# Non-local attention block: row products made over fewer steps, the next image's first products ended earlier, and left sums taken with transposes

## What is computed

```
x4  = groupnorm(x)                       # per image, 32 groups
g_x = g_w @ x4 + g_b                     # 128 x 4096
f   = x4.T @ x4                          # 4096 x 4096, symmetric
y   = softmax(f, axis=-1) @ g_x.T
wy  = W_w @ y.T + W_b                    # 256 x 4096
wy  = batchnorm(wy over all 4 images) * gamma + beta
out = x + wy + x4
```

## Time and profile before

| | before |
|---|---|
| median of 3 runs | 2225.02 us (2223.76 to 2226.59) |
| profiled execution's own time | 2227.25 us |
| its span, first to last instruction | 2225.5 us |
| mean granted TensorE clock | 0.982 of full speed |
| TensorE busy | 2082.0 us, 94% of the span |
| VectorE, ScalarE, GpSimd busy | 69%, 49%, 37% |

### The profile page before, as it was taken

One profiled execution on the slowest core, in us unless ns is written; L12 is line 12 of the kernel. 1 busy time (PEld: TensorE's weight loads), 2 busy tenths in 40 slices (PEclk: granted clock), 3 DMA queues, 4 the chain that ended last, 5 costly groups with the idle time before them and its releaser, 6 DMA issues.

```text
span 2225.5 us, 32504 instructions
## 1 busy us (share of the span) xinstructions
PE 2082.0 (94%) x9460; PEld 1487.4 (67%) x9460; DVE 1527.1 (69%) x3095; ACT 1096.3 (49%) x2234; POOL 813.5 (37%) x624
## 2 busy tenths in 40 slices
PE   5899999999999999999999999998999999999988
PEld 4687776755687777665668677675658777666433
DVE  5576666777766766686766666677776677667656
ACT  3344545556444444546544454555544444454645
POOL 3002223459502023447730222355950102345750
PEclk9999999999999999999999999999999999999989
DMA  3112233555512323464531223455541132336969
GB/s 137 76 76 87 99 114 128 166 152 166 185 45 90 112 74 109 142 199 133 174 106 78 86 100 114 128 175 155 172 167 62 72 119 90 119 119 222 333 234 359
DMA packets 108410, 304.53 MB, mean 137 GB/s; under 512 B 11584, under 2 KB 11968, under 8 KB 93888
## 3 DMA queue, kind: packets, MB, share of 16 engines
q1 hardware_dynamic: 108224, 302.30, 39.7%
HBM read 159.65 MB, written 142.61 MB: 136 GB/s over the span
## 4 chain that ended last, share of the span: by engine, by line
PE 67%; issue 11%; POOL 10%; DVE 4%; ACT 4%; DMA 3%; SPq 0%; DVEq 0%; POOLq 0%; ACTq 0%
PE bank L1199 11%; PE bank L1133 9%; PE bank L1135 9%; PE bank L1134 9%; PE bank L1175 8%; PE bank L1203 4%; PE bank L1205 4%; PE bank L1204 4%; POOL fy_d L694 4%; POOL fy_c L694 3%; PE bank L1349 3%; ACT ring L760 2%; PE bank L1270 2%; DMA fy_d<-spill 2%; POOL xl L667 2%
## 5 line engine op out<-in xcount | busy, mean ns | idle before, releaser
L786 ACT CAST phi<-bank 128x512 fp32r<-128x512 f32 x480 | 280.8, 587 | 779.0 <-PE bank L1175 778.4
L930 DVE TENSOR_SCALAR_CACHE_REDUCE ring<-bank 128x512 f32<-128x512 f32 x576 | 395.9, 687 | 245.2 <-PE bank L1135 200.4
L1133 PE MATMUL bank<-xh 128*128 128x512 f32 (+3 forms) x1152 | 521.2, 452 | 7.3 <-POOL xl L667 6.4
L1135 PE MATMUL bank<-xh,xl 128*128 128x512 f32 (+3 forms) x1152 | 439.1, 381 | 0.0
L965 DVE TENSOR_TENSOR plo<-bank,phi 128x512 fp32r<-128x512 f32 x480 | 325.7, 684 | 161.7 <-ACT phi L786 123.7
L1134 PE MATMUL bank<-xl,xh 128*128 128x512 f32 (+3 forms) x1152 | 436.4, 379 | 0.0
L1175 PEld LDWEIGHTS bank<-ident,ring 128*128 128x128 f32 x1920 | 233.6, 142 | 199.4 <-issue 130.0
L1175 PE MATMUL bank<-ident,ring 128*128 128x128 f32 x1920 | 295.5, 277 | 61.4 <-DVE plo L965 31.2
L760 ACT ACTIVATE ring<-ring,nmax 128x512 f32<-128x512 f32 x480 | 344.7, 720 | 0.0
L694 POOL TENSOR_TENSOR fy_c<-fy_c,maxrow 128x512 f32<-128x512 f32 x200 | 261.9, 1312 | 146.9 <-DMA fy_c<-spill 146.5
L694 POOL TENSOR_TENSOR fy_d<-fy_d,maxrow 128x512 f32<-128x512 f32 x188 | 243.0, 1295 | 190.4 <-DMA fy_d<-spill 190.3
(11 more groups left out here) (115 smaller groups left out, 2720.7 us busy)
## 6 DMA issues: line engine op xcount, KB each, us to landing
spill<-ring SPq DMA_DIRECT2D x112, 1024.0 KB, 4.4
fy_c<-spill SPq DMA_DIRECT2D x200, 256.0 KB, 4.6
fy_d<-spill SPq DMA_DIRECT2D x188, 256.0 KB, 4.2
ring<-x_dram SPq DMA_DIRECT2D x40, 512.0 KB, 4.6
lbuf<-spill SPq DMA_DIRECT2D x60, 256.0 KB, 3.8
yd<-yn SPq DMA_DIRECT2D x32, 256.0 KB, 3.4
fx_a<-x_dram SPq DMA_DIRECT2D x16, 512.0 KB, 8.6
out_dram<-fx_a SPq DMA_DIRECT2D x16, 512.0 KB, 5.4
```

What stands on the lines that cost most here:

```text
L786: nc.scalar.copy(phi[:, HI_BUF[n], :], whole(p)).then_inc(hi_made, 1)
L930: last = nc.vector.tensor_scalar(ring[:, SLOT[u], t, :], src, 1.0, None, ALU.mult, ALU.max, accum_out=rowm[:, t, c:c + 1])
L1133: nc.tensor.matmul(dst, xh[:, k, rows], xh[:, k, cols], start=(k == 0), stop=False)
L1135: last = nc.tensor.matmul(dst, xl[:, k, rows], xh[:, k, cols], start=False, stop=(k == K - 1))
```

## The change

Three things, and a part that follows from them:

- `plan_products` makes the products of block 2 in 19 steps in place of 25 (in block 1's steps), and those of blocks 3, 4 and 5 in 18. Blocks 1, 6 and 7 stay. As a result the last product of block 2 stands at step 1.21 (before 1.24), of block 3 at 2.17 (2.24), of block 4 at 3.21 (3.23), of block 5 at 4.17 (4.22); maxima are merged at 1.23, 2.19, 3.23, 4.19 (before 1.26, 2.26, 3.25, 4.24). Some steps hold two products: 1.03, 1.05, 1.14 to 1.18, 2.02, 2.08, 3.12, 3.13 (before: 1.14 to 1.16).
- `plan_exps` is not edited, but its bound moves: the four exponentials that stood together at 1.28 and 2.28 (three and one at 3.27 and 3.28) now stand one in each of the steps 25 to 28. The copy of the spread maxima (`take_maxrow`) moves from 1.29 to 1.26, from 2.29 to 2.27 and from 3.28 to 3.27.
- `NEXT_TO` is 239 in place of 245: the 32 products of the next image's row 0 stand at 181, 182, 184, ... 237, 239 (before 181, 183, 185, ... 242, 245), two of them moved from block 7 to block 6, and their maxima are merged at 7.16 (7.22). The sends to `spill` of their chunks move along; the one of chunk (0, 7) stands at 7.16 in place of 7.22.
- `sum_left` transposes the four 128 x 128 pieces of `lsb` against `ident` (128 columns each) in place of multiplying them by a 128 x 2 tensor of ones, and `invert` reduces the 128 x 512 result on VectorE into `lside` before it adds. The tensor `ones` and its memset go.

```diff
-        steps = range(PRODUCTS_FROM[j], PRODUCTS_FROM[j] + (25 if j < 6 else 2 * n))
+        steps = range(PRODUCTS_FROM[j], PRODUCTS_FROM[j] + {1: 25, 2: 19, 3: 18, 4: 18, 5: 18, 6: 2 * n, 7: 2 * n}[j])
...
-NEXT_AT, NEXT_TO = XN_STEP[0] + 5, TILES - 11
+NEXT_AT, NEXT_TO = XN_STEP[0] + 5, TILES - 17
...
-                    nc.vector.tensor_tensor(lsum[:, :], sps[:, 0:2 * T].rearrange("p (t o) -> p t o", o=2)[:, :, 0],
-                                            lsum[:, :], ALU.add).then_inc(summed, 1)
+                    nc.vector.tensor_reduce(lside[:, :], sps.rearrange("p (t m) -> p t m", t=T), AX.X, ALU.add
+                                            ).then_inc(side_summed, 1)
+                    dve.wait_ge(side_summed, b * (NB - 1) + j)
+                    nc.vector.tensor_tensor(lsum[:, :], lside[:, :], lsum[:, :], ALU.add).then_inc(summed, 1)
...
-                    last = nc.tensor.matmul(sps[:, 2 * t:2 * t + 2], lsb[:, t * P:(t + 1) * P], ones[:, :],
-                                            start=True, stop=True)
+                    last = nc.tensor.transpose(sps[:, t * P:(t + 1) * P], lsb[:, t * P:(t + 1) * P], ident[:, :])
```

More of the change, by code:

```diff
@@ L421, in nonlocal_block @@
         gavg = sb("gavg", [P, P])
-        ones = sb("ones", [P, 2])
         wgs = sb("wgs", [P, K, 2 * CI], F32R)
@@ L439, in nonlocal_block @@
         lsum = sb("lsum", [P, T])
+        lside = sb("lside", [P, T])
         linv = sb("linv", [P, T])
@@ L494, in nonlocal_block @@
         left_summed = sem("left_summed")
+        side_summed = sem("side_summed")
         summed = sem("summed")
@@ L698, in _ @@
             nc.gpsimd.memset(neghalf[:, :], -0.5)
-            nc.gpsimd.memset(ones[:, :], 1.0)
             nc.gpsimd.memset(ident[:, :], 0.0)
```

## The result

| | before | after |
|---|---|---|
| median beside each other | 2225.81 us (4 runs) | 2195.49 us (4 runs, 2194.60 to 2196.57) |
| ratio, 95% interval | | 0.9859 (0.9838 to 0.9880) |
| profiled execution's own time | 2227.25 us | 2195.28 us |
| its span | 2225.5 us | 2193.5 us |
| mean granted clock | 0.982 | 0.991 |

The change makes the kernel 1.4% faster, and the median is within 1 us of the predicted 2196.0. That it is so close is luck: the sum behind it was -29.2 us, the two profiled executions are 32.0 us apart and the two medians 30.3, and single terms of the sum were off by 3 to 5 us in opposite directions, as the point-by-point part shows. Each ratio is an estimate over the executions with its interval, and can differ from the quotient of the two medians by up to 0.001, or 2 us.

What follows compares the result with a forecast made beforehand. TensorE, 94% busy, was taken as the bound. Left sums with inverse -7.8, block ends -16.4, packed steps +2, clock -11, image ends +4 sum to -29.2: 2198.0 profiled, 2196 beside the median; forecast 2184 to 2207, wider range 2170 to 2216.

Steps and rivals of the forecast that it cites:

- What bounds the kernel: TensorE, 94% busy; time is won only where it does less, stands idle, or has a low clock.
- Ends of blocks: Steps 25 to 31 of blocks 1 to 3: holes fall from 7.6 to 3.5 us an image, -16.4 us.
- The rival that ScalarE bounds the longer ends: At block ends holes return in small pieces; only 8 us of holes and 4 of clock won, 2211; chance 0.14.
- Left sums: At 28 left sums, transposes take 0.45 us where ones and their matmul take 0.90: -12.6 us on TensorE.
- the rival by which transposes are no cheaper: Left sums: transposes pay by 128 columns, ones by 2; 12.6 us lost from the sum, 2208; chance 0.04.
- The inverse: VectorE's 0.75 us reduction delays it at step 5.01 of three images, +3.6, and in the last image's tails, +1.2.
- Packed steps: Products packed into earlier steps: VectorE at 79% holds, runs late only at 1.18 and 1.19; +2 us, 0 to +8.
- the slower rival: VectorE becomes the bound in the packed stretches, TensorE losing 0.7 us per doubled step; 2237; chance 0.07.
- Clock: Low clock behind five of twelve ends of blocks cost about 15 us; 11 come back, -11, between 0 and -17.
- Image ends: Steps 7.24 and 7.30: one hole of some 3 us; three ends, +1 holes and +3 clock, +4 us.
- The rival that everything closes: At block ends holes go but for the merge's wait, clock stays up, also at image ends; 2175; chance 0.12.
- that it does nothing: Holes move from ends to packed stretches one for one, clock falls as often; 2221; chance 0.05.

Runs made afterwards that it cites:

- kernel 1: Kernel before with only the left sums by transposes and VectorE's reduction; 2213.63 us, ratio 0.9960.
- kernel 5: Changed kernel with the exponentials of blocks 2 to 5 held back to the steps they had before, products still packed; 2211.17 us, ratio 0.9933.
- Kernel 9: Changed kernel with the products of blocks 3, 4 and 5 in 14 steps and block 2 in 15; 2203.24 us, ratio 0.9889.
- kernel 2: Kernel before with only the products of blocks 2 to 5 in 18 or 19 steps; 2200.96 us, ratio 0.9899.
- kernel 4: Changed kernel with the next image's row of products ending at step 245 again; 2196.59 us, ratio 0.9880.
- kernel 6: Changed kernel with the left sums of blocks 4 and 5 by ones again, transposes for the rest; 2198.76 us, ratio 0.9881.
- Kernel 8: Changed kernel with VectorE adding one column of the transposed sum in place of the reduction; 2189.94 us, ratio 0.9841.
- kernel 12: Changed kernel with the left sum's reduction on ScalarE and the next image's row ending at 245; 2206.13 us, ratio 0.9899.
- 3: Kernel before with only the next image's row of products ending at step 239; 2227.76 us, ratio 1.0015.
- 11: Changed kernel with the left sum's reduction on ScalarE, row ending at 239; 2210.66 us, ratio 0.9916.
- 7: Changed kernel with ones for the left sums of blocks 4 and 5 and the next image's row at 245; 2194.82 us, ratio 0.9857.
- 10: Changed kernel with the products of blocks 2 to 5 in 22 steps; 2198.06 us, ratio 0.9857.

## Why the prediction was right, point by point

The four images' steps take 31.7 us less between the two profiled executions (0.3 of the 32.0 lies outside). Added up step by step, with clock and gaps taken apart, they divide as follows. A block with a low clock is compared with the same block of an image without one, or, where there is none, at half the low time. The gaps are TensorE's idle time in a step. What remains is 7.8 us. The left sums are put at 28 x 0.45 in it, the price of one in the chain, which kernel 1 bears out (its blocks 2, 3 and 4 are 0.43 to 0.46 us shorter than before's with the same gaps), and the 4.8 the other way is what is left over.

| | predicted | measured |
|---|---|---|
| idle time in blocks 1, 2, 3 (holes at their ends) | -16.4 | -18.6 |
| left sums, TensorE's work | -12.6 | -12.6 |
| inverse later: blocks 5 and 6, last image | +3.6 and +1.2 | +4.5, +1.6, -1.8 |
| packed steps, short waits | +2 | +4.8 |
| gaps in block 7 and in block 0 | +1 | +1.3 and +1.8 |
| low clock | -11 and +3 | -12.8 |
| sum | -29.2 | -31.8 (rounded terms) |

*What bounds the kernel: right.* The gain is where the three views put it. TensorE's share of the span is still 94%.

*Ends of blocks: right, a little too careful.* 3.5 us of holes an image were expected to stay and 2.75 did, 1.35, 1.07 and 0.32 against 1.0, 1.7 and 0.8. The holes by themselves gave 20.0 us for the 16.4; the table's 18.6 has 1.3 us of new short gaps among the packed steps taken off. ScalarE at 14.62 us of work beside 17.13 was hidden better than I gave it credit for; kernel 5 shows that the spacing did it. What is left in block 1 is the pair in the chain above.

*The rival that ScalarE bounds the longer ends* falls with this: it needed 8 us or less to be won. Kernel 9 speaks against it too: its end of block 2 is three steps longer without products and its holes are the same; what it loses, it loses in the packed steps.

*Left sums: the transposes' price right, to the hundredth.* 0.44 and 0.23 against 0.79 and 0.34. In blocks 3 and 4 the changed kernel takes 56.8 and 55.9 us, the products alone 57.3 and 56.4. With it falls the rival by which transposes are no cheaper. The Trainium skill's page "TensorE: Matmul & The Clock Gate", section "Back-to-back issue gap", has fewer columns the cheaper. Here four products of 128 x 2 took 0.79 and four transposes of 128 columns 0.44, so for this pair the measurement decides against it. The products are eight passes and the transposes four (x8 and x4 in the chain), 0.10 and 0.11 us each: it is the number of passes that makes the ones dearer, and the columns hardly count.

*The inverse: right at 5.01, incomplete elsewhere.* The slack of 0.50 was used up and 1.37 stood in its place; block 5 grew 1.5 us, of which kernel 2 (58.8 to 59.1, against 58.3) puts 0.5 or more on the products and the rest on the sum. I hadn't seen that step 6.01 would wait too, nor the 0.45 an image at steps 0.12 and 0.13, whose cause I did not follow. The 1.24 at 6.01 comes with the row's end at 239; with 245 (kernel 4) it is 0.34. It cost nothing that kernel 6 could give back: GpSimd is busy 52.38 of block 6's 58.10 us, and its pace is the likely bound there. I had priced the reduction at 0.75, but the addition behind it takes 0.50 where it took 0.15, and the chain from its start to the inverse is 1.44 us in place of 0.37, 1.07 more. Kernel 8 prices the whole at 4 to 6 us, the prediction had 3.6 + 1.2. In the last image the spreads wait 1.4 us more (1.2 foreseen); that its blocks 5 to 7 idle 1.8 less all the same is other gaps, 3.2 us, that closed and stood in no term.

*Packed steps: too small.* The doubled steps take 3.4 to 4.07 us and none waits for VectorE but 2.02, by 0.17, so the slower rival (VectorE bound at 79%) falls; 37.2 of 47.3 us was foreseen and 36.76 of 47.40 came. Yet 0.2 to 0.6 us a block are lost in blocks 1 to 4 in matmuls that stand a little longer than their 0.23, too short to show as a gap: in block 4, which has no holes in either kernel, the products alone give 56.4 where before has 56.0. So this term was mis-sized, 4.8 for 2, or 6.1 with the short gaps (0.2 behind step 1.05, 0.17 at 2.02), inside its bounds (0 to +8).

*Clock: right in kind, 4.8 us too small.* All of it came back at the ends of blocks, not 11 of 15: the five pieces of the earlier trace rows cost 13.7 us, by the same blocks of other images, and a sixth near the end of the last image's block 0, which is not among those rows, 1.7 more.

```profile
1756.90:1760.30 3.40, 3.40 (x15) 3.01 (x14) 0.91 (x2) 1.61 (x5) 0.00 (x0) 0.50 0.00 0
```

The ends of images took 2.6 us back, at one of three, near the 3 that I had put down. One more thing wasn't in the prediction: before also has a low clock of 3.4 us early in each block 6 (504.2, 1036.7 and 1558.9), which is gone after, but saved nothing. The window of block 6 of image 1, before:

```profile
1034.90:1091.60 56.70, 55.64 (x201) 34.95 (x199) 41.28 (x82) 33.36 (x58) 52.19 (x38) 0.97 0.52 172
```

and with the products alone, where no low clock falls there:

```profile
1018.30:1075.00 56.70, 54.62 (x200) 33.80 (x199) 41.28 (x82) 33.44 (x58) 52.10 (x38) 1.00 0.52 172
```

56.70 us both times. TensorE only waits 1 us more when it is faster; GpSimd, busy 52 us of it, is the likely bound. So this low clock cost nothing. That is not so for every one in this block: in kernel 12, where TensorE waits longer at its start, block 6 takes 58.5 us with 3.4 us of low clock and 57.3 without, with GpSimd busy 52.3 in both.

*Image ends: the form right.* "As one hole of some 3 us": 2.78. In the eight profiles with the row at 239 (after and kernels 3, 5, 6, 8 to 11) the low clock fell on 13 of 24 image ends, in the six with 245 (before and kernels 1, 2, 4, 7, 12) on none of 18. The holes are 3.7 to 3.9 against 3.2 to 3.4. The time leans against 239: in the three pairs on one chip (before and 3, 7 and 6, 12 and 11) the row ending at 245 is the faster by 3.3, 3.9 and 4.5 us, the first within the interval of no change. Only kernel 4, on another chip than the changed kernel, leans the other way (0.9880 against 0.9859), within the intervals. So this part of the change brought nothing that shows and may cost some 4 us. Blocks 6 and 7 together take 110.4 us in place of the 110.8 of kernel 4, since two products moved from the one to the other.

*The rival that everything closes* (2175) falls by the 2.75 us of holes that stay in an image; *that it does nothing* by the ratio.

Four versions stand level with the changed kernel within the noise (kernels 4, 6, 7 and 10), none clearly beyond it. The 4 to 6 us of the reduction are what is left, and ScalarE at the next block's first step isn't the place for it. Whether a place later in the block would do was not tried.

## What to carry to other kernels

When an engine in strict order feeds another, look at how its long instructions are bunched before looking at how busy it is: four exponentials in a row cost TensorE 1.2 to 1.3 us more at each block's end than the same four one to a step (kernel 5 against the changed kernel), with ScalarE at 77 and 80% load behind the products of block 2. Before moving a small piece of work to an engine with time to spare, look at what stands ahead of it in that engine's queue; the busy share hides a wait of 3.4 us. And before pricing a low clock, look whether TensorE bounds the stretch: one cost nothing in block 6 of before, another 1.2 us in the same block of kernel 12.

## What the runs showed of the hardware

A hole of 2 us or less was enough to be followed by a low clock in before at some places and not at others of the same form: the ends of blocks in image 2 are the same as in image 1 and kept 1.00, where those of image 1 lost it for 10.3 and 6.8 us. With the left sums by transposes alone (kernel 1) the pieces at the same holes were 3.4 us long, in one profile. And four full matmuls of float32 with 2 columns (eight passes) took longer than four transposes of 128 columns (four passes), 0.79 against 0.44 us; a pass took 0.10 and 0.11.
